# Normalisation order, bf16 ranks and slot table, and unread dense products on TensorE

## The reference, cut to what matters

```python
x = x + gnn(_layernorm(x), edge_index, edge_type, edge_weight, ...)   # graph attention, 8 heads of 64
x = x + ffn(_layernorm(x)[None], ...)[0]                              # mixture of experts
# ffn, with xt the 1250 rows, E = 64 experts, K = 2, hidden size 256:
scores = sigmoid(xt @ Wg.T + bg)
w, idx = top_k(scores, 2);  w = w / w.sum(-1, keepdims=True)
nx  = normalise(xt)
h   = silu(nx @ W1p[e] + b1p[e]) * (nx @ W3p[e] + b3p[e])   # for the two experts e of each row
y   = sum over its two experts of w * (h @ W2[e] + b2[e])
z   = (silu(nxs @ Ws1 + bs1) * (nxs @ Ws3 + bs3)) @ Ws2 + bs2   # shared expert, all rows
x   = x + y + z
```

## Time and profile before

| | |
|---|---|
| median of three runs | 751.66 us (750.05 to 753.65) |
| the profiled execution | 749.77 us, of which the span of the trace is 748.0 |
| TensorE busy | 612.7 us (82% of the span) |
| VectorE, ScalarE, GpSimd busy | 486.6, 234.5, 263.0 us |
| HBM | 184.31 MB read, 16.58 MB written |

### The profile page before, as it was taken

The page is one execution under the profiler, slowest core; times in us unless marked ns, Lnnn a source line. Parts: engine busy times, 40 slices in busy tenths (PEclk is TensorE's granted clock), DMA queues, the critical chain, the costliest instruction groups (busy, mean ns, idle before and its releaser), DMA issues. The chain is left out here.

```text
span 748.0 us, 9448 instructions
## 1 busy us (share of the span) xinstructions
PE 612.7 (82%) x3091; PEld 297.1 (40%) x3091; DVE 486.6 (65%) x950; ACT 234.5 (31%) x575; POOL 263.0 (35%) x281
## 2 busy tenths in 40 slices
PE   2979996534999999999089999999999999998940
PEld 2645665522333333333077453443333333332310
DVE  5886778897999999998777745533233333332307
ACT  1563554514755443435276210111111111111110
POOL 3000005775777777778400011222222222222210
PEclk9898998655999999999655999999999999998985
DMA  8433667866779977795721007999999999999929
GB/s 258 122 82 100 158 157 240 252 182 174 209 211 336 361 227 211 212 371 177 273 85 56 1 19 276 397 379 409 414 414 412 409 414 411 380 379 414 364 79 364
DMA packets 68135, 194.30 MB, mean 260 GB/s; under 512 B 14539, under 2 KB 15621, under 8 KB 68086
## 3 DMA queue, kind: packets, MB, share of 16 engines
q1 hardware_dynamic: 37270, 100.70, 37.2%
q0 software_dynamic: 19600, 56.41, 23.9%
q10 hardware_dynamic: 11216, 36.58, 12.6%
HBM read 184.31 MB, written 16.58 MB: 269 GB/s over the span
## 5 line engine op out<-in xcount | busy, mean ns | idle before, releaser
L599 POOL DMA_INDIRECT y_rows<-nxb,slot_tab x33 | 34.3, 1040 | 193.1 <-ACT nxb L784 191.2
L1711 DVE TENSOR_TENSOR nxb<-ps,nxb 128x256 f32<-128x256 f32 (+1 forms) x33 | 14.0, 424 | 134.3 <-PE ps L1075 73.1
L569 POOL DMA_INDIRECT nxb<-h_rows,srcx x50 | 47.5, 951 | 128.8 <-DMA h_rows<-ring 108.9
L1075 PE MATMUL ps<-arena,nxb 128*64 128x512 f32 x352 | 82.1, 609 | 0.0
L569 POOL DMA_INDIRECT ring<-h_rows,srcx x74 | 71.0, 960 | 23.5 <-issue 20.7
L969 PE MATMUL ps<-ring,edge 128*128 128x512 f32 x148 | 67.3, 603 | 7.4 <-issue 6.8
L825 PE MATMUL ps<-ident,nxb 128*128 128x128 f32 (+1 forms) x248 | 49.5, 321 | 20.3 <-ACT nxb L731 19.7
L825 PEld LDWEIGHTS ps<-ident,nxb 128*128 128x128 f32 (+1 forms) x248 | 39.2, 207 | 65.2 <-issue 57.7
L1088 PE MATMUL ps<-arena,nxb 128*64 128x512 f32 x260 | 63.9, 604 | 0.9 <-DVE nxb L1714 0.9
L1445 DVE TENSOR_TENSOR xn<-ps,xn 128x512 f32 x88 | 60.9, 692 | 2.4 <-PE ps L969 1.5
L781 ACT ACTIVATE nxb<-ps 128x256 f32<-128x256 f32 (+1 forms) x33 | 12.7, 384 | 155.5 <-PE ps L1075 155.5
(11 more groups left out here) (300 smaller groups left out, 1047.0 us busy)
## 6 DMA issues: line engine op xcount, KB each, us to landing
arena<-in_L_ffn_W_dram SPq DMA_DIRECT2D x47, 1024.0 KB, 12.4
arena<-in_L_ffn_W_dram ACTq DMA_DIRECT2D x29, 1024.0 KB, 10.4
edge<-in_L_ffn_W_dram SPq DMA_DIRECT2D x20, 1024.0 KB, 12.6
arena<-edge_keys SPq DMA_DIRECT2D x22, 320.0 KB
ring<-y_rows SPq DMA_DIRECT2D x9, 512.0 KB, 6.9
ring<-edge_keys SPq DMA_DIRECT2D x10, 320.0 KB
h_rows<-ring SPq DMA_DIRECT2D x10, 256.0 KB, 2.0
nx_rows<-nxb SPq DMA_DIRECT2D x10, 256.0 KB, 2.0
```

Source lines behind the costliest of these rows:

```text
L569: pool.indirect_dma_start(out=slot(k), out_offset=None, in_=h_d[:, :], in_offset=bass.IndirectOffsetOnAxis(ap=srcx[:, k:k + 1], axis=0)).t ...
L599: pool.indirect_dma_start(out=y_d[:, :], out_offset=bass.IndirectOffsetOnAxis(ap=at, axis=0), in_=yo[:, u, :], in_offset=None, bounds_chec ...
L1075: o = pe.matmul(ps[c, 2 + k, :], xgT[:, k, a, c], w13[b][:, x, :, a, :], start=False, stop=(a == A - 1), skip_group_check=True)
```

## The change

1. On VectorE `gnn_sum` of a step goes ahead of `x1_scale`.
2. TensorE gets `dense(n)`: n fp32 products of the identity with itself, 512 columns wide, into bank 4. Nothing reads them. Five stand ahead of the first group of the normalisation and two ahead of each later one.
3. `hits` is bf16 and laid out [P, NEX, NT], and one scan along the tiles replaces the ten additions; a mask `within`, 0 at each expert's first tile, ends the sum there. The rank products are bf16 and split by experts, 48 and 16.
4. The one-hot matrices of the slot table are bf16. The payload is split in two: the part within a tile, by VectorE (`tile_lo`), and 256 times the tile's number, by nine operations on ScalarE (`tile_hi`); the table is 20 + 18 bf16 products.
5. `shared_up` is cut into halves with banks of their own (`UP_BANKS`) and waits of their own (`UP_FREE`). Half (0, 0) goes ahead of the rank products and half (0, 1) after; `shared_down(0)` and `(1)` go behind the slot table, half (3, 0) follows them, and half (3, 1) goes into `BESIDE[0]`, behind the first expert pair. `shared_hidden` and `shared_add` on VectorE move accordingly, one place later each.

```diff
-    BESIDE = {2: (("up", 4),), 3: (("cw", 0), ("cw", 1)), ...
+    BESIDE = {0: (("half", 3),), 2: (("up", 4),), 3: (("cw", 0), ("cw", 1)), ...
+    UP_BANKS = ((4, 5), (1, 2), (4, 5), (3, 5), (1, 7), (1, 7))
+    UP_FREE = ((0, 0), (0, 0), (1, 1), (0, 3), (4, 4), (5, 5))
...
+                    if n == 1:
+                        act.wait_ge(s("route_step"), 2)
+                        for t in range(1, NT):
+                            o = act.activation(tile_hi[:, 2 * t:2 * t + 2, :], tile1h[:, 2 * t:2 * t + 2, :], ACT.Identity,
+                                               scale=2.0 * P * t)
+                        o.then_inc(s("tile_hi"), 1)
...
+            def shared_half(k, w):
...
+                if UP_FREE[k][w]:
+                    pe.wait_ge(s(("act_sh", "hs_done")[w]), UP_FREE[k][w])
+                for a in range(A):
+                    o = pe.matmul(ps[:, UP_BANKS[k][w], 0:c], ws13[:, w, a, m * P:(m + 1) * P],
+                                  xT[:, a, c0:c1], start=(a == 0), stop=(a == A - 1))
+                o.then_inc(s("pe_sh1" if w == 0 else "pe_sh3"), 1)
...
+            def dense(n):
+
+                for i in range(n):
+                    pe.matmul(ps[:, 4, :], ident[:, :], ident[:, :].unsqueeze(1).to_broadcast([P, 4, P]), start=True, stop=True)
+
             pe.wait_ge(s("param_done"), 1)
             for t0, t1 in LNG:
+                dense(2 if t0 else 5)
                 for t in range(t0, t1):
                     nx_turn(t)
                 for t in range(t0, t1):
                     logits(t)
             pe.wait_ge(s("sh_in"), 16 * 9)
-            shared_up(0)
-
-            pe.wait_ge(s("before_done"), 1)
...
+            shared_half(0, 0)
+
+            pe.wait_ge(s("lg_read"), NT)
+            pe.wait_ge(s("route_step"), 1)
+            for n, (e0, e1) in enumerate(RANKS):
+                o = ps[:, 6 + n, 0:(e1 - e0) * NT]
+                pe.matmul(o, tri_b[:, :], hits[:, e0:e1, :].rearrange("p e t -> p (e t)"), start=True, stop=False)
+                pe.matmul(o, ones_b[:, :], upto[:, e0:e1, :].rearrange("p e t -> p (e t)"), start=False, stop=True)
+            pe.matmul(ps[:, 7, 3 * NEX:4 * NEX], ones_b[:, :], upto[:, :, NT - 1], start=True, stop=True).then_inc(s("pe_rank"), 1)
+            shared_half(0, 1)
             shared_up(1)
             shared_up(2)
-            pe.wait_ge(s("lg_read"), NT)
+
+            pe.wait_ge(s("route_step"), 3)
+            for k in range(2 * NT):
+                pe.matmul(ps[:, 0, 0:NCOL], rank1h[:, k, :], tile_lo[:, k, :], start=(k == 0), stop=False)
+            pe.wait_ge(s("tile_hi"), 1)
+            for k in range(2, 2 * NT):
+                o = pe.matmul(ps[:, 0, 0:NCOL], rank1h[:, k, :], tile_hi[:, k, :], start=False, stop=(k == 2 * NT - 1))
+            o.then_inc(s("pe_slots"), 1)
             pe.wait_ge(s("hs_done"), M)
             shared_down(0, SPARE[1])
             shared_down(1, SPARE[0])
...
-            shared_up(3)
+            shared_half(3, 0)
...
             for step in range(G + 4):
+                if step < G:
+                    gnn_sum(step)
                 if 0 <= step - 2 < G:
                     x1_scale(step - 2)
-                if step < G:
-                    gnn_sum(step)
...
-            for t in range(NT):
-                link(v.tensor_tensor(before[:, t + 1, :], before[:, t, :], hits[:, t, :], ALU.add))
...
+            link(v.tensor_tensor_scan(upto.rearrange("p e t -> p (e t)"), within.rearrange("p e t -> p (e t)"),
+                                      hits.rearrange("p e t -> p (e t)"), 0.0, ALU.mult, ALU.add))
```

More of the change, by code:

```diff
@@ L88, in gnn_moe_kernel @@
     SKIP = 1 << 20
[L90 to L91 removed]
+    BESIDE = {0: (("half", 3),), 2: (("up", 4),), 3: (("cw", 0), ("cw", 1)), 4: (("up", 5),), 5: (("cw", 2),), 6: (("down", 3),),
+              7: (("down", 4),), 8: (("down", 5),), 10: (("down", 6),), 11: (("down", 7),), 12: (("down", 8),), 14: (("down", 9),)}
+    UP_BANKS = ((4, 5), (1, 2), (4, 5), (3, 5), (1, 7), (1, 7))
+    UP_FREE = ((0, 0), (0, 0), (1, 1), (0, 3), (4, 4), (5, 5))
     DOWN0 = 3
@@ L326, in gnn_moe_kernel @@
         onehots = Carver(nxb[:, :, :].rearrange("p t d -> p (t d)"), NT * D)
-        rank1h = onehots([P, 2 * NT, P])
-        tile1h = onehots([P, 2 * NT, NCOL])
+        rank1h = onehots([P, 2 * NT, P], BF16)
+        tile1h = onehots([P, 2 * NT, NCOL], BF16)
+        tile_lo = onehots([P, 2 * NT, NCOL], BF16)
+        tile_hi = onehots([P, 2 * NT, NCOL], BF16)
+        iota_b = onehots([P, P], BF16)
+        rank_b = onehots([P, 2 * NT], BF16)
+        tile_b = onehots([P, 2 * NT], BF16)
+        pay_b = onehots([P, 2 * NT], BF16)
         lg = router([P, NT, NEX])
@@ L332, in gnn_moe_kernel @@
         tmp = router([P, NT, 2, NEX])
-        hits = router([P, NT, NEX])
-        before = router([P, NT + 1, NEX])
+        hits = router([P, NEX, NT], BF16)
+        upto = router([P, NEX, NT], BF16)
+        within = router([P, NEX, NT], BF16)
+        tri_b = router([P, P], BF16)
+        ones_b = router([P, P], BF16)
         eidx = sb("eidx", [P, NT, 2])
@@ L996, in logits @@
                 o.then_inc(s("pe_lg"), 1)
-            def shared_up(k):
+            def shared_half(k, w):
                 n, m = k // M, k % M
@@ L1003, in shared_up @@
                 pe.wait_ge(s("nxs_done"), A * (n + 1))
-                for w, read in ((0, "act_sh"), (1, "hs_done")):
-                    if k:
-                        pe.wait_ge(s(read), k)
-                    for a in range(A):
-                        o = pe.matmul(ps[:, 4 + w if k < 4 else SPARE[w], 0:c], ws13[:, w, a, m * P:(m + 1) * P],
-                                      xT[:, a, c0:c1], start=(a == 0), stop=(a == A - 1))
-                    o.then_inc(s("pe_sh1" if w == 0 else "pe_sh3"), 1)
+                if UP_FREE[k][w]:
[4 more added lines that the diff above has]
+                o.then_inc(s("pe_sh1" if w == 0 else "pe_sh3"), 1)
+            def shared_up(k):
+                shared_half(k, 0)
+                shared_half(k, 1)
             def shared_down(t, bank):
@@ L1024, in _ @@
             pe.wait_ge(s("sh_in"), 16 * 9)
-            shared_up(0)
-            pe.wait_ge(s("before_done"), 1)
-            for t0, t1 in ((0, 8), (8, NT)):
-                o = ps[:, 6 + t0 // 8, 0:(t1 - t0) * NEX]
-                pe.matmul(o, tri[:, :], hits[:, t0:t1, :].rearrange("p t e -> p (t e)"), start=True, stop=False)
-                pe.matmul(o, ones[:, :], before[:, t0:t1, :].rearrange("p t e -> p (t e)"), start=False, stop=True)
-            pe.matmul(ps[:, 7, 2 * NEX:3 * NEX], ones[:, :], before[:, NT, :], start=True, stop=True).then_inc(s("pe_rank"), 1)
+            shared_half(0, 0)
[7 more added lines that the diff above has]
+            shared_half(0, 1)
             shared_up(1)
             shared_up(2)
-            pe.wait_ge(s("lg_read"), NT)
+            pe.wait_ge(s("route_step"), 3)
[5 more added lines that the diff above has]
+            o.then_inc(s("pe_slots"), 1)
             pe.wait_ge(s("hs_done"), M)
@@ L1038, in _ @@
             shared_down(1, SPARE[0])
-            pe.wait_ge(s("onehots"), 1)
-            for k in range(2 * NT):
-                o = pe.matmul(ps[:, 0, 0:NCOL], rank1h[:, k, :], tile1h[:, k, :], start=(k == 0), stop=(k == 2 * NT - 1))
-            o.then_inc(s("pe_slots"), 1)
-            shared_up(3)
+            shared_half(3, 0)
             def aside(j):
-                for name, count in (("zh_added", DOWN0 + beside(j, "down")), ("hs_done", 4 + beside(j, "up")),
+                for name, count in (("zh_added", DOWN0 + beside(j, "down")), ("hs_done", 3 + beside(j, "half") + beside(j, "up")),
                                     ("cwT_done", beside(j, "cw"))):
@@ L1054, in aside @@
                         shared_up(k)
+                    elif kind == "half":
+                        shared_half(k, 1)
                     elif kind == "down":
@@ L1740, in _ @@
                 for n, (kind, k) in enumerate(BESIDE.get(j, ())):
-                    if kind == "up":
+                    if kind in ("up", "half"):
                         shared_hidden(k)
```

65 lines of the change are left out of this document (38 added, 27 removed).

## The result

| | before | changed |
|---|---|---|
| median | 750.41 us (748.88 to 753.65, 6 runs) | 741.39 us (737.91 to 745.3, 6 runs) |
| ratio | | 0.9874, 95% interval 0.9838 to 0.991 |
| profiled execution | 749.77 us, span 748.0 | 741.96 us, span 740.2 |
| on a second chip (5 rounds) | 834.94 | 822.23, ratio 0.9859 (0.9818 to 0.9901) |
| on a third (5 rounds) | 751.72 | 741.32, ratio 0.9866 (0.9833 to 0.9898) |

The change gains 9.0, 12.7 and 10.4 us between medians; the ratios are taken over the fast executions alone, so they are not the ratios of these medians.

The account below looks back on a forecast made before the run. It took an engine chain up to the first expert product, then DMA bandwidth, as the bounds: 14.2 us earlier there, less 1.8 us idle DMA, makes -12.4 us from 751.66, so 739.3 us; overall range 735 to 747.

Parts of the forecast that it names:

- What bounds: Whole kernel: a chain over several engines bounds up to the first expert product, then DMA; an earlier start moves the end.
- 1, the order: Normalisation: gnn_sum fits in VectorE's wait for ScalarE's spread, bringing the fifth group's spread 4.15 us earlier.
- 2, the dense products: Normalisation groups: they hold TensorE at full clock at no cost; the first shared product starts 5.5 us earlier.
- second rival: Clock falls once or twice, for instance after waits at 398 and 403 us, costing 3.4 to 6.8 us; chance 0.18.
- 3, the ranks: Ranks: scan 1.5 us, hits 0.8 to twice that, products 0.6 us from 404.8; VectorE goes on 11.5 us earlier.
- 4, the table: Slot table: products start at 423.4, take 1.6 us instead of 4.42; the first expert product comes 14.2 us earlier.
- a sign of being wrong: After the slot table's inputs: TensorE or ScalarE waiting for VectorE past 423 us would refute the prediction.
- 5, the half between the pairs: Head of the expert stream: half (3, 1) delays the second pair, and DMA idles about 1.8 us more.
- The sum: Whole kernel: -14.2 us at the first expert product plus 1.8 us of idle DMA gives -12.4 us.
- last sign: End of the weight stream: the last load must land as much earlier as the first was issued.

Follow-up runs that it names:

- Run 2: The kernel before with only gnn_sum moved ahead of x1_scale; ratio to before 0.9942.
- run 1: The changed kernel without its dense products; ratio to before 0.9874.
- run 7: The changed kernel with rank masks made in VectorE's wait for the fifth spread, one dense product behind the last logits, and hits written with a stride; ratio to before 0.9877.
- run 6: The kernel before with the dense products and one more in TensorE's wait for ScalarE's scaling; ratio to before 0.999.
- run 8: The changed kernel with halves (3, 0) and (3, 1) behind the first and second expert pairs, one dense product in the scaling wait, masks moved; ratio to before 0.9852.
- run 4: The changed kernel with half (3, 1) ahead of the experts instead of behind the first expert pair; ratio to before 0.9884.
- run 9: The changed kernel with half (3, 1) behind the third expert pair, later asides moved back, one dense product in the scaling wait, masks moved; 737.54 us, ratio to before 0.9804.
- third trace of the changed kernel: The changed kernel unchanged, run again on the third chip beside the kernel before; 741.32 us, ratio to before 0.9866.
- second of before: The kernel before, unchanged, traced again on the third chip; ratio to before 1.0012.
- second trace of the changed kernel: The changed kernel unchanged, run again on the second chip; 822.23 us, ratio to before 0.9859.
- run 3: The kernel before with the dense products and nothing else; ratio to before 0.9965.

## Why the prediction was right

**What bounds** held for the large shifts. Run 2 moved the first two expert products by 4.3 us and the end by 3.9 to 4.1 (the last product's clock taken out); the changed kernel moved the first by 14.6 and 13.4 and the end by 10.7 and 11.3. Shifts of 1 to 2 us do not come through so cleanly: in run 1 both products are 1.6 us later and the end between 0.3 earlier and 0.2 later, in run 7 they are 2.3 later and the end 0.8 to 1.3, and in run 6 they are earlier and the end is later. What starts the first one alone does not move the end (run 8).

**1, the order**: 4.15 us forecast, 4.2 measured, alone and in the whole.

**2, the dense products**: they held the clock in the groups, as forecast, but this is worth 1.6 us of the 13.4 to 14.6. What the working left out is that a group at half clock, without dense products, fits the new period too (run 1), and that VectorE's chain sets the ranks. Of the rule of the Trainium skill (TensorE: Matmul & The Clock Gate, Part 4: PE-mode transpose) that transposes do not bring the full clock, no run here tells more than the earlier trace rows did. The second rival, one fall of the clock, happened in the profiled execution (401.4 to 405) and cost nothing, because VectorE's ranks were last there: 69.36 us to the first expert product with the fall, 69.30 and 69.38 in the traces without it. This was close: the half product took 5.37 us instead of 3.67, and TensorE then waited 0.36 us for the ranks instead of 2.0. The prediction had said that a fall costs half its length where TensorE is the bound, and then priced the rival as if TensorE always were.

**3, the ranks**: `hits` 1.57 us instead of 0.8, which was the upper bound; the rank products stand 0.7 us later than forecast for that, and cost 0.82 us instead of 0.6. The 0.6 does not follow from its own row either: 30 products of 80 columns in 1.25 us make 0.85 us of 1632 columns, and 0.70 of the 1344 that the five products have by their sizes.

**4, the table**: the forecast of 423.4 was met at 423.5, and this is luck. The working lets the rank products start at 404.8 and VectorE go on at 405.6, and then lets TensorE begin with the same rank products at 405.6: it counts them twice. From 404.8, its own 17.8 us end at 422.6. The 0.7 us by which the ranks were late and the 0.2 us more that they cost filled that gap; the five half products took 17.17 us, 17.2 forecast. The margin to VectorE was forecast as 0.7 us and was nearly nothing: `tile_lo` (L1688) ended at 424.96, the table products began at 425.02. ScalarE did wait for VectorE behind that point (2.72 us, to 425.72, for the buffer `sil`), which the prediction had named as a sign of being wrong, but no piece of the chain waits for it. `tile_hi` took 2.01 us for nine copies, below the bound of 3.6. That bf16 one-hots cost as much as fp32 held. It agrees with what the Trainium skill (VectorE: DVE Perf Modes, What auto-detection actually checks) asks for two results a cycle, 16-bit tensors with step 1 throughout, which the repeated operand is not; no run here takes that operand away.

**Items 3 to 5 of the change have no run of their own**, but for half (3, 1) in run 4 (3.7 us at the first expert product, 2.1 at the second). Runs 1 and 2 shared a chip, had no dense products, and differ by these three items alone: 7.4 us at the first expert product (70.97 against 78.41 us), half of the whole gain. Of it the chain shows 1.5 us at the rank products (0.82 us for 2.34) and 3.0 at the table (1.40 for 4.42); the rest is not separated.

**5, the half between the pairs**: 1.8 us of idle DMA forecast, 1.5 to 1.8 measured in the windows; run 9 gets them back.

**The sum**: 14.2 forecast, 14.6 (first traces) and 13.4 (one chip, third traces) at the first expert product; less 1.5 to 1.8 of DMA, 11.6 to 13.1; at the end 10.7 and 11.3 from the first spread. The prediction's last sign was that the last load lands as much earlier as the first was issued. The chain of before and then of the changed kernel (first traces) has these rows, start and length of the last load and of the last read of results in each:

```profile
695.07 16.82 DMA edge<-in_L_ffn_W_dram
...
734.07 9.50 DMA ring<-y_rows
```
```profile
683.22 18.67 DMA edge<-in_L_ffn_W_dram
...
724.29 10.15 DMA ring<-y_rows
```

From the first spread the load lands at 347.3 and at 335.8 us, 11.5 us earlier, where the first expert product was 14.6 earlier: 3.1 us are lost on the way. Of these, 1.8 are the head of the stream, which the prediction had counted; 1.3 us are not explained. The last read took 0.65 us more. In the third trace of the changed kernel one more loss can be seen: an expert product of 6.43 us at half clock (clock 0.71 from 602.4 to 612.4 us) and a DMA share of 0.83 in the 10 us behind it. So the size of the stream's term was right at its head and too small over the whole stream, and the forecast gain of 12.4 us is 2.0 and 3.4 us above the medians' 10.4 and 9.0 (the second chip, with no trace of before, has 12.7).

The rest stands ahead of the first spread. Between the profiled executions the gain is 7.8 us (first) and 10.3 (third against the second of before), for the first spread came 1.5 and 2.6 us later in the changed kernel, and the last product's clock takes 1.5 us in the one and gives 1.6 in the other. The trace shows one place, though not why: TensorE's timeline at 17 us, of the kernel before and then of the changed one (first trace), in a part of the program that the change does not touch.

```profile
17.93 3.88 PE L841 MATMUL ps<-arena 128*128 128x16 f32 x32
```
```profile
17.20 6.85 PE L859 MATMUL ps<-arena 128*128 128x16 f32 x32
```

These 32 took 3.88 and 4.07 us in the two traces of before; 6.85 us in the first and the third of the changed kernel and in run 8; 3.7 to 4.0 in all other runs, run 9 and the second trace of the changed kernel among them. Whether it belongs to the change or to chance, three of nine against none of five cannot tell, and no run was made for it. Nor is it the whole of the delay: run 9, with 3.78 us there, has its first spread at 368.73 us, as late as run 8's 368.60 with 6.85.

## What to carry to other kernels

Ask of a clock that fell what was last at that place: while another engine sets the pace, half speed on TensorE costs little or nothing (1.6 us over the five groups in run 1, nothing from 401.4 to 405), and full speed bought by extra products can be given back at the first wait behind them (run 3). Where loads are released by products some steps back, the head of the stream has to keep its pace too: look at the DMA share of the first 10 us windows, and put work that has to go somewhere behind the step at which the stream has work in hand, not between the first two. And time an edit from an anchor in its own trace, since here the stages ahead of it moved by as much as a quarter of the gain. A total that comes out right is no proof of its terms: here two errors of some 0.8 us each cancelled in the middle of the sum, and only the table of steps shows it.

## What the runs showed of the hardware that was not expected

- A VectorE addition of 640 elements from fp32 to bf16 took 1.57 us with strided reads and 3.01 us with a strided write.
- The clock fell behind waits of 1.40 us (first trace of the changed kernel) and of 0.34 and 1.06 us (runs 4 and 6), and held through the same 1.41 (its second trace) and 0.33 and 1.06 (both traces of before and run 9). The length of the wait alone does not tell.
- ScalarE copied 144 bf16 elements in 0.22 us (nine such copies in 2.01 us).
- Two of the chips took 77 to 89 us more to the first spread (445 to 454 us against 365 to 369) and no more for the rest.
